# Preparing the experts' weights without a pause at the next batch's normalisation, one chunk in five units instead of four

## What is computed

```python
xn = layernorm(x)                       # (4, 1024, 512)
q, k, v = (xn @ W.T + b for W, b in ...)  # 16 heads of 32
p = softmax(where(causal, q @ k.T / sqrt(32), -inf) - slope[h] * |i - j|)
attn = (p @ v) @ Wo.T + bo
top2, sel = top_k(softmax(xn @ gate_w.T), 2); top2 /= sum(top2)
g, u = split(xn @ w1[e].T)              # 8 experts, w1: (8, 704, 512)
moe = sum_e combine[e] * ((silu(g) * u) @ w2[e].T)   # w2: (8, 512, 352)
out = x + attn + moe
```

## Time and profile before

| | us |
|---|---|
| median of 3 runs | 1560.26 (1558.79 to 1565.82) |
| the profiled execution | 1556.29 |
| its span, first to last instruction | 1554.5 |
| units 0 to 511 | 50.1 to 1091.0 |
| units 70 to 105 of batches 0, 1 | 174.1 to 250.7, 441.4 to 517.9 |
| TensorE busy | 1423.9 |
| VectorE busy | 1013.7 |
| ScalarE busy | 882.3 |
| GpSimd busy | 566.6 |
| mean granted TensorE clock | 0.98 |

### The profile page before, as it was taken

One profiled execution on the slowest core, in us unless ns is written; L12 is line 12 of the kernel. 1 busy time (PEld: TensorE's weight loads), 2 busy tenths in 40 slices (PEclk: granted clock), 3 DMA queues, 4 the chain that ended last, 5 costly groups with the idle time before them and its releaser, 6 DMA issues.

```text
span 1554.5 us, 37269 instructions
## 1 busy us (share of the span) xinstructions
PE 1423.9 (92%) x13659; PEld 924.0 (59%) x13659; DVE 1013.7 (65%) x2462; ACT 882.3 (57%) x1994; POOL 566.6 (36%) x595
## 2 busy tenths in 40 slices
PE   4899979998997999989899898999999999999995
PEld 2576656665665666666565566675466556556663
DVE  7887887666878777777788977788343333333331
ACT  5677777665778767776776465777122222222221
POOL 4111232121123213113312233132237777777764
PEclk9999999999999999999999999999999999999998
DMA  7355232433423255453114233145978788888883
GB/s 267 101 141 138 87 108 65 126 102 106 135 85 115 79 150 155 135 157 89 61 61 128 82 105 81 54 150 158 340 152 136 126 133 135 130 143 145 137 131 46
DMA packets 171357, 193.40 MB, mean 124 GB/s; under 512 B 87536, under 2 KB 121072, under 8 KB 171056
## 3 DMA queue, kind: packets, MB, share of 16 engines
q1 hardware_dynamic: 143760, 151.67, 35.6%
q0 software_dynamic: 26128, 37.24, 14.5%
q10 hardware_dynamic: 1296, 2.11, 0.4%
HBM read 93.45 MB, written 53.74 MB: 95 GB/s over the span
## 4 chain that ended last, share of the span: by engine, by line
PE 67%; DVE 11%; issue 7%; ACT 5%; SPq 3%; DMA 3%; POOL 3%; DVEq 0%; ACTq 0%; POOLq 0%
PE S L1240 16%; PE O L1177 7%; PE T L1161 5%; PE S L1150 5%; PE T L1118 4%; PE O L1271 4%; PE M L1271 4%; DVE arena L1544 4%; SPq L993 3%; PE M L1118 3%; PE S L1161 2%; PE M L1161 2%; PE S L1118 2%; PE T L1202 2%; ACT arena L1736 2%
## 5 line engine op out<-in xcount | busy, mean ns | idle before, releaser
L1736 ACT ACTIVATE arena<-arena,mneg 128x1024 f32<-128x1024 f32 (+7 forms) x512 | 395.3, 772 | 72.1 <-DVE mneg L1544 70.4
L1544 DVE CUSTOM_DVE_ANT_0 arena<-S,cF,nsl 128x1024 f32<-128x1024 f32 (+7 forms) x512 | 408.9, 806 | 23.3 <-PE S L1150 14.2
L1240 PE MATMUL S<-arena 128*128 x1704 | 265.6, 312 | 2.0 <-DVE arena L1655 2.0
L1892 POOL DMA_INDIRECT out<-arena x142 | 222.7, 1568 | 105.3 <-issue 43.2
L1150 PE MATMUL S<-arena 96*128 96x512 f16 (+3 forms) x768 | 210.7, 329 | 18.8 <-DVE mneg L1544 17.4
L1240 PEld LDWEIGHTS S<-arena 128*128 128x128 f16 x1704 | 166.3, 98 | 98.2 <-issue 2.8
L1161 PE MATMUL T<-cF,arena 128*128 128x128 f32 x1198 | 199.1, 277 | 24.6 <-DVE arena L1560 13.4
L1177 PE MATMUL O<-arena 128*32 128x128 f32 (+1 forms) x3328 | 176.4, 327 | 13.6 <-DVE arena L1575 13.6
L1753 ACT ACTIVATE arena<-T 128x512 f32<-128x512 f32 (+3 forms) x258 | 118.6, 463 | 109.6 <-PE T L1161 108.7
L1161 PEld LDWEIGHTS T<-cF,arena 128*128 128x128 f32 x1198 | 140.4, 141 | 67.3 <-issue 24.6
L1669 DVE COPY arena<-T 128x512 f16<-128x512 f16 x71 | 30.2, 425 | 213.7 <-PE T L1255 213.7
(11 more groups left out here) (207 smaller groups left out, 2322.5 us busy)
## 6 DMA issues: line engine op xcount, KB each, us to landing
arena<-arena SPq DMA_DIRECT2D x192, 128.0 KB, 2.5
arena<-in_w1T SPq DMA_DIRECT2D x64, 352.0 KB, 3.4
arena<-in_x SPq DMA_DIRECT2D x64, 256.0 KB, 3.4
w_d<-arena SPq DMA_DIRECT2D x32, 352.0 KB, 2.9
arena<-w_d SPq DMA_DIRECT2D x16, 704.0 KB, 6.8
arena<-in_w2T SPq DMA_DIRECT2D x32, 256.0 KB, 2.8
out<-arena SPq DMA_DIRECT2D x32, 256.0 KB, 2.9
xn_d<-arena SPq DMA_DIRECT2D x24, 256.0 KB, 2.0
```

The costliest lines, as they stand in the source:

```text
L1240: tp = pe.matmul(y[:, i * 512:i * 512 + I], xT[:, s % XDEEP, 4 * a + c, :], weights[:, bass.ds(reg[s] + (w_ * NX * W1N + c * 2 * I + i * I ...
L1544: dve.tensor_tensor_reduce(ring[r][:, 0:w], SBK[o.bank["score", u]][:, 0:w], rel[:, S - w:S], nsl[:, hh:hh + 1], 3.0e38, ALU.add, ALU.min, ...
L1736: act.activation(ring[r][:, 0:w], ring[r][:, 0:w], ACT.Exp, bias=mneg[:, m:m + 1], scale=-1.0, accum_out=rs[:, k, c:c + 1]).then_inc(sems[ ...
L1892: pool.indirect_dma_start(out=halves, out_offset=bass.IndirectOffsetOnAxis(row[:, part, s:s + 1].bitcast(U32), 0), in_=yo[:, s % YDEEP, c0 ...
```

## The change

Two edits. The condition that leaves out units 70 to 105 of batches 0 to 2 goes, and `w_split` has one more step between the high and the low half, so that a chunk takes five units.

```diff
@@ w_split
             add("wsh", i)
             load["act"] += 0.8
+            yield
             yield
             add("wsl", i)
             load["dve"] += 0.9
@@ the loop over units
-        if u >= 4 and not (u < 128 * (B - 1) and 70 <= u % 128 < 106):
+        if u >= 4:
             while split_jobs and next(split_jobs[0], jobs) is jobs:
                 split_jobs.pop(0)
```

## The result

The changed kernel took 1590.97 us (median of 4 runs, 1588.22 to 1593.01) against 1563.04 us of the kernel before (4 runs, 1558.79 to 1566.45): a ratio of 1.0158, 95% interval 1.0135 to 1.0181. It is slower, as forecast, but by about 28 us and not 15, and 1591 lies above the range of 1561 to 1588. The profiled execution took 1588.22 (span 1586.4), 31.9 more than that of before.

A forecast was written before the change was run, and what follows sets the result against it. In units 88 to 95 VectorE was taken as full, so the change puts work where its engines are the bound. Terms 12.1 - 8.7 + 9.2 + 4.6 + 6.2 - 2.1 - 6.0 = +15.3 us gave about 1575 us, range 1561 to 1588.

The forecast's parts named there:

- units 88 to 95, three batches: Pauses of batches 0 to 2: VectorE is full there, so the inserted work is paid whole, +5.7 us.
- units 80 to 87: Pauses: 0.7 over VectorE's room and 1.7 for a late chunk in batch 0, 1.0 over ScalarE's in batch 1; +3.4 us.
- scales leave unit 152: Units 152 to 159: VectorE's wait for the all-reduce of the maxima goes from the old place, -8.7 us.
- scales at unit 116: New place: ScalarE waits 11.6 us for GpSimd's subtraction behind the all-reduce; +9.2 us, between 3 and 12.
- store wait at unit 154: Batch 1, second group: ScalarE's split waits 8.6 us for a store behind the stacking DMAs; +6.2 us.
- store wait at unit 254: Batch 2, first group: ScalarE's wait for a store behind the stackings becomes 7.8 us; +4.6 us.
- batch 3 relieved: Splits end at unit 402 instead of 455, relieving units 362 to 455; -6.0 us, between 2 and 20.
- a cover of 2.4 us: Part of a wait on another engine that TensorE does not feel, from 8.7 us waited and 6.3 idle.
- The lag covers it: Rival: transposes four units behind the scores cover 8.2 us of each wait, so not slower, 1556 us; 14%.
- One load, not two: Rival: GpSimd's 7.2 us behind the all-reduce are paid elsewhere or not at all; ScalarE waits 4.4, 1568.4 us; 12%.
- The inserts are serial: Rival: all work put into the pauses costs both engines' time, 36.5 us for 12.1, total 1600 us; 6%.
- Batch 3 was bound by both engines: Rival: each of 13 removed splits in units 403 to 455 gives both engines' time, 20 us, total 1561.6; 10%.

The follow-up runs named there:

- the kernel that holds the splits: Changed kernel, a split held until seven units after a stacking when the store ahead of it stands one to three units behind that stacking: 1579.14 us.
- holds of 9.75: Kernel before, with spare copies on ScalarE in units 44, 172, 300, 112 and 240, holding it 3.2, 6.5, 9.75, 9.75 and 3.2 us: 1597.53 us.
- the shortened kernels: Changed kernel, side work of units 78 to 87 on 32 columns, transfers whole: both engines 1587.46 us, ScalarE's part alone 1596.10, VectorE's alone 1588.68.

## Why the forecast was wrong in size

By its own terms, with what the same stretches of the two profiled executions give:

| term | forecast | measured |
|---|---|---|
| units 88 to 95, three batches | +5.7 | +5.3 |
| units 80 to 87 | +3.4 | +14.7 |
| units 96 to 103 | +3.0 | +4.3 |
| scales leave unit 152 | -8.7 | -8.2 |
| scales at unit 116 | +9.2 | +10.4 |
| store wait at unit 154 | +6.2 | +8.4 |
| store wait at unit 254 | +4.6 | +1.8 |
| unit 312 | -2.1 | -2.9 |
| batch 3 relieved | -6.0 | -1.5 |
| sum | +15.3 | +32.3 |

The two entries at unit 152 and 154 are parted with the kernel that holds the splits (16.8 us without either wait, 25.0 and 25.2 with one of them). The spans differ by 32.0 us: the stretches that no term names took 2.7 us less, and the part behind unit 511, which no term names either, 2.1 more. The last row counts units 362 to 455.

**Units 80 to 87: the failed step, 11 of the 17 us missing.** The forecast priced them by what VectorE and ScalarE had room for (0.93 of the time), 0.7 and 1.0 us over, and gave the meeting with the stackings "between nothing and 3.5 us, taken as 1.7" in batch 0 and nothing in the others: 3.4 us in all, and it measured 14.7. With the work shortened the stretches stayed at 20.5, 20.0 and 19.2 us, so room was the wrong measure; with nothing put behind the stackings of unit 77 and its like in batches 1 and 2, 7 us of batch 0, 3 of batch 1 and 1 of batch 2 went. In batch 0 the trace shows the way: VectorE stands in front of the late chunk, and the store of normalised rows waits behind what is put on SyncE's queue. In batch 1 the trace shows a store of a split behind the stacking, 2.84 us of ScalarE's time and 3.50 of TensorE's. The forecast had that very mechanism, but its list of meetings (units 151, 180, 252, 279, 312, 378) leaves out the stackings in the pauses, which no split had met before. It is not the whole of it: with that wait gone only 0.8 us came back. How the rest of batches 1 and 2 divides among store, load, the split's own place and the moved copies was not told apart. That SyncE issues both the stackings and the stores of the normalised rows was in the code; the forecast followed the queue for the stores of splits and not for the rows being normalised.

**The clock: missing in the long terms.** The forecast took a cover of 2.4 us off each wait, from the earlier trace rows, and gave the clock no term. Its own row showed it: in the earlier trace rows the stretch with the wait has TensorE busy for 18.78 us at 0.86, the one without for 16.40 at 1.00. The full 8.7 us were lost there, cover or not: 6.3 idle and 2.4 at the lower level. Most long waits measured since cost nearly their length: 11.0 us cost 10.4 (VectorE's wait for the all-reduce, inside it, had its own part in that), 8.9 cost 8.4, holds of 9.75 cost 10.2 and 11.2, one of 6.5 cost 5.2. Two cost less, both behind the stacking of unit 250: 8.7 cost 5.8 (the kernel with its splits five units later) and 6.83 cost 2.8 (unit 256, against the kernel with the hold; the same splits took up to 1.6 us less in other executions). Why these two were covered better stays open. With 2.4 us of lower clock on top, the entries of 9.2 and 6.2 would have been 11.6 and 8.6. Over the whole kernel the 15.1 us by which TensorE's busy time exceeds fit that reading; no run sums them up.

**The relief of batch 3.** "About half" of TensorE's 9.1 us of idleness was a guess between 2 and 20; units 403 to 455 gave nothing (125.3 and 125.2), and without the last 13 splits 0.9. The 1.5 us of the table came ahead of them. VectorE's share of 77% was no bound, and falling to 70% it freed no one.

**Right:** the scale's term. ScalarE waited 11.04 us for L1839 (11.6 forecast), and a use one unit behind the all-reduce cost 8 to 10 us at units 116, 135 and 152, though only 3.6 at unit 125; six units behind cost nothing at unit 152. The two store waits came at units 155 and 256 with 8.90 and 6.83 us (8.6 and 7.8 forecast). At the second the loss was 1.8 and not 4.6: it had the better cover told of above. Units 88 to 95 came out at 14.1, 14.5 and 15.5 us (15.4, 14.7 and 14.3); that their sum fits is in part luck, since one is 1.3 too low and another 1.2 too high. No experiment shortened the work there, so that its reason, VectorE being full, stays argued. Units 152 to 159 did not come to 22 us but to 25.2.

**The rivals.** *The lag covers it* is out for the whole, though a part of it holds: of the wait of 6.83 us some 4 were covered; 8.9 and 11.0 cost nearly their length once the clock is counted. *One load, not two* is out: the 7.00 us stand in the trace, and 6.90 where nobody waited. That it is a load is not shown; the trace has only the time. "GPSIMD Engine Reference" of the Trainium skill, section 2.1, speaks of the first call alone; the trace agrees on that one (6.39) and shows a second of the same size on the way back, which the page does not name. *The inserts are serial* gave 1600 and came nearest in size, but for a cause that the shortened kernels refute in units 80 to 87. *Batch 3 was bound by both engines* is out by 124.3 against 125.3.

## What to carry to other kernels

Before work is put where engines look free, follow the queue its transfers go through, and ask which transfer of the main chain stands behind them there: eight units without side work behind a burst of twelve DMAs gave back 11 of the 15 us that units 80 to 87 had lost. The total went back to that of before, but 19 of its 30 us are where the later jobs happened to move. A shift of side jobs by a few units was itself worth 6 to 10 us a stretch here, in either direction, so compare stretch by stretch. A wait of about 9 us on an engine that feeds TensorE is safest priced at its full length here, since the clock mostly takes back what the lag of the pipeline had covered; one of 3 us cost 0.6 to 1.6. And where an engine is slow to answer, as GpSimd is with the all-reduce, leave several units between the question and the use: here that alone made the kernel 0.5 to 0.6% faster.

## What the runs showed of the hardware

- GpSimd's all-reduce is paid twice in time that no instruction shows: 5.6 to 6.4 us ahead of it, and 6.6 to 8.0 us ahead of the next TENSOR_TENSOR. A CAST between the two runs at once (0.46 us, no wait, in the kernel before with six units behind the all-reduce).
- Behind the gaps that the scale (3.17 and 4.73 us) and the store of unit 155 (5.99 us) opened on TensorE, it runs at 1.2 GHz for a while, which adds about 2.4 us: windows of units 112 to 127 at a clock of 0.88 with 36.0 us busy, against 33.5 at 1.00. In units 80 to 87 of batch 1, where shorter gaps (0.6, 3.50 and 0.8 us) follow each other, it added up to 3.0 us to idle time grown by 2.7.
- Twelve stacking DMAs hold SyncE for 7.7 to 9.1 us; a store or load of a 704-wide chunk behind them takes it 0.6 us (490.09 and 490.73 in the changed kernel).
- Units 0 to 15 take 27.5, 30.7 or 31.7 us from one execution to the next; in the longer cases the granted clock falls to the lower level once more between 50 and 56 us. Why was not looked into.
